# Causal attention with its scores made twice: once for the row maximum, once keys by queries with the maximum as two extra rows

## The chip, the core and the metric

One core of one Trainium2 chip runs the whole program. The core has five engines with queues of their own: PE (matrix products), DVE (vector), ACT (scalar), POOL and SP (here only a queue that starts DMAs). The metric is device time in microseconds (us); the median of three runs of the kernel before is 2293.73 us (2292.71 to 2295.2).

## The reference, cut to what matters

```python
def xattn(q, latent_kv, Wq, Wkv_expand, Wout):      # b=8, sq=512, H=512, 16 heads of 32
    qp = q @ Wq.T
    k, v = jnp.split(latent_kv @ Wkv_expand.T, 2, axis=-1)
    ...
    scores = jnp.einsum('bhqd,bhkd->bhqk', qh, kh) / sqrt(32)
    scores = jnp.where(tril, scores, finfo.min)      # causal
    attn = jax.nn.softmax(scores, axis=-1)
    return merge_heads(attn @ vh) @ Wout.T
x = x + xattn(layernorm(x), ctx_512, ...)
x = x + ffn(layernorm(x), ...)    # router of 8 experts per output column, top two, then the experts
```

Because of the causal mask only the first 512 of the 1601 context tokens matter. All is float32.

## The kernel before

The program has two stages. Attention runs first over 8 batches and stores x1; the router and the experts then run over 32 blocks of 128 tokens. The change touches the attention alone.

**Tiling.** A batch b has four chunks c of four heads each (128 of the 512 features); chunk n = 4b + c. A chunk has eight units v: unit v treats query block i = v // 2 (128 queries, keys 0 to 128(i+1), so 128 to 512 columns) of head pair v % 2. Per chunk PE makes the queries (Q, 4 x 3 products of 512 columns, L423) and the keys (K, 3 products, L434) as a high and a low float32r part, which ACT and DVE split (L693, L951). SP stacks the parts by 12 DMAs (`stack`, L280) into `qk_st`, so that one product over 96 rows gives the score to near float32 accuracy.

**One unit.** PE makes the scores of two heads, queries on partitions, and adds the mask by a product of bf16 tiles (L526, L529); two pairs of PSUM banks take turns. DVE takes the negated row maxima (L1021). ACT makes the exponentials with that maximum as its bias and with a running sum, one instruction a head (L740). Two units later (LAG) PE turns the probabilities, 128 x 128 at a time (`turn_probs`, L475), and ACT and DVE copy one head each into `pT` (L708, L968). When all eight units of chunk n-1 are turned, at unit v = 2 of chunk n, PE multiplies by the values (`values_of`, L486): four column tiles of 32 side by side, float32 in both operands. The reciprocals of the sums are taken on 16 numbers a partition (L974), spread to 512 (L978), turned by PE (L451), copied by ACT (L760) and multiplied in by DVE (`scaled`, L987). POOL splits the result (L1367, L1369).

**Order.** Every engine's queue is written out by hand and is in order. `fillers` (L238) says which other PE work stands in which unit: K at v = 0, Q at v = 1, the turned reciprocals R at v = 2; values V (3 products each) in chunk 0 at v = 4 to 7, the output projection WO (12 products each) in chunk 1 at v = 4 to 7, the turned layer norm LNT in chunk 2 at v = 4 to 7. K and Q are those of chunk n+1. `over_batches` (L261) writes batch 0 and batch 7 out and runs batches 1 to 6 in a hardware loop, so the loop is turned five times.

## Time and profile before

| | |
|---|---|
| median of three runs | 2293.73 us |
| the profiled execution | 2295.15 us, span 2293.1 us |
| attention, to the last product with values | about 0 to 720 us |
| PE busy over the span | 2173.1 us (95%) |
| DVE, ACT, POOL busy | 69%, 49%, 31% |
| mean granted TensorE clock | 0.986 |

Times in the rows are from the start of the span. Busy time of PE counts the latency of each product, so neighbouring products overlap in it; the pace is read from start to start. An idle time in brackets names who ended it; "issue" is a wait for nothing that the profile shows. A clock of 1.00 is 2.4 GHz, the other level is 1.2 GHz.

### The profile page before, as it was taken

The numbers are of one execution on the slowest core, as the hardware profiler recorded it, in microseconds if no ns is written. First come the engines' busy times: TensorE is split into PE (matmuls) and PEld (weight loads), VectorE is DVE, ScalarE is ACT, GpSimd is POOL, SyncE is SP. The second block draws the span as 40 slices with busy tenths as digits, with TensorE's granted clock in tenths as the row PEclk, the third lists the DMA queues.
The fourth block names the chain that finished last, engine by engine and source line by source line (L and its number), as shares of the span: only waits on it lengthen the run. The fifth ranks groups of instructions, "written<-read, shape, count | busy, mean of one in ns | idle before, by whom it ended". The sixth has DMA issues, their size and how long they took to land.

```text
span 2293.1 us, 37558 instructions
## 1 busy us (share of the span) xinstructions
PE 2173.1 (95%) x11264; PEld 1685.4 (73%) x11264; DVE 1591.9 (69%) x2844; ACT 1123.6 (49%) x3059; POOL 710.0 (31%) x669
## 2 busy tenths in 40 slices
PE   5998898998998999999999999987999999999999
PEld 4676676776775777777777777766888888888887
DVE  4775666756767899999999999997633434333433
ACT  4766656657666577777777777783200000000000
POOL 1330321312302465666556665652200000000000
PEclk9999999999999999999999999998999999999999
DMA  5444444435436000000000000040000000000000
GB/s 147 118 109 119 116 99 106 123 91 124 97 100 218 19 10 9 9 14 9 9 11 12 9 9 14 9 151 11 26 21 27 18 27 18 27 18 27 18 27 19
DMA packets 64106, 123.08 MB, mean 54 GB/s; under 512 B 8553, under 2 KB 8577, under 8 KB 64033
## 3 DMA queue, kind: packets, MB, share of 16 engines
q1 hardware_dynamic: 64032, 122.28, 19.6%
q8 instruction: 24, 0.39, 0.1%
q14 instruction: 50, 0.40, 0.1%
HBM read 55.12 MB, written 16.78 MB: 31 GB/s over the span
## 4 chain that ended last, share of the span: by engine, by line
PE 53%; DVE 19%; issue 18%; ACT 7%; DVEq 1%; SPq 1%; DMA 1%; POOL 0%; ACTq 0%; POOLq 0%
PE pair L227 11%; PE pair L229 11%; PE pair L228 11%; DVE ps L1209 4%; PE ps L475 4%; PE ps L486 3%; DVE top_b L1121 3%; PE ps L227 3%; ACT probs L740 3%; PE ps L228 3%; PE ps L229 3%; PE pair L526 2%; DVE top_b L1139 2%; DVE top_a L1131 2%; DVE scrap L1217 1%
## 5 line engine op out<-in xcount | busy, mean ns | idle before, releaser
L227 PE MATMUL pair<-w_h,hT_h 128*128 128x512 f32 x2048 | 855.1, 418 | 4.4 <-issue 2.7
L229 PE MATMUL pair<-w_h,hT_l 128*128 128x512 f32 x2048 | 803.1, 392 | 0.0
L228 PE MATMUL pair<-w_l,hT_h 128*128 128x512 f32 x2048 | 798.1, 390 | 0.0
L1296 DVE SCALAR_TENSOR_TENSOR xb<-pair,c_now,xb 128x512 f32<-128x512 f32 x256 | 192.1, 751 | 398.5 <-PE pair L229 398.0
L229 PEld LDWEIGHTS pair<-w_h,hT_l 128*128 128x128 f32 x2048 | 385.1, 188 | 86.8
L228 PEld LDWEIGHTS pair<-w_l,hT_h 128*128 128x128 f32 x2048 | 386.2, 189 | 80.4
L227 PEld LDWEIGHTS pair<-w_h,hT_h 128*128 128x128 f32 x2048 | 388.3, 190 | 75.5 <-issue 5.1
L1438 POOL TENSOR_TENSOR logits<-logits,second 128x512 f32<-128x512 f32 x256 | 323.5, 1306 | 134.2 <-DVE second L1153 134.2
L783 ACT ACTIVATE hT_h<-ps 128x512 fp32r<-128x512 f32 x64 | 38.3, 599 | 664.7 <-PE ps L583 664.7
L1377 POOL TENSOR_TENSOR rstd<-moments,eps 128x1 f32<-128x1 f32 x96 | 77.2, 804 | 844.3 <-DVE moments L924 844.3
L740 ACT ACTIVATE probs<-pair,nmax 128x384 f32<-128x384 f32 (+3 forms) x512 | 272.8, 556 | 33.5 <-DVE nmax L1021 33.5
L1021 DVE TENSOR_REDUCE nmax<-pair 128x2 f32<-128x256 f32 (+3 forms) x256 | 210.0, 820 | 83.7 <-PE pair L529 82.8
L475 PE MATMUL ps<-ident,probs 128*128 128x128 f32 x1280 | 194.2, 282 | 31.3 <-ACT pT L708 28.9
L1367 POOL TENSOR_TENSOR oT_h<-o_sb,zero 128x512 fp32r<-128x512 f32 x32 | 33.3, 1039 | 531.6 <-DVE o_sb L987 310.3
L708 ACT ACTIVATE pT<-ps 128x128 f32<-128x128 f32 (+3 forms) x256 | 118.9, 464 | 147.2 <-PE ps L475 124.7
L968 DVE COPY pT<-ps 128x128 f32<-128x128 f32 (+3 forms) x256 | 124.2, 485 | 96.1 <-PE ps L475 96.1
L526 PE MATMUL pair<-qk_st 96*128 96x384 f32 (+3 forms) x512 | 163.1, 377 | 24.4 <-ACT probs L740 13.7
L475 PEld LDWEIGHTS ps<-ident,probs 128*128 128x128 f32 x1280 | 138.5, 143 | 47.9 <-issue 34.2
L846 ACT ACTIVATE logits<-pair 128x512 f32<-128x512 f32 x256 | 145.3, 583 | 29.2 <-PE pair L229 29.1
L1209 DVE SCALAR_TENSOR_TENSOR ps<-logits,ps 128x512 f32<-128x512 f32 x217 | 148.9, 686 | 3.7 <-POOL logits L1438 0.4
L1217 DVE SCALAR_TENSOR_TENSOR scrap<-ps,w 128x512 bf16<-128x512 f32 x217 | 145.0, 678 | 0.0
L803 ACT ACTIVATE over<-logits 128x512 f32<-128x512 f32 x224 | 133.1, 623 | 15.3 <-POOL logits L1438 15.2
(150 smaller groups left out, 3176.2 us busy)
## 6 DMA issues: line engine op xcount, KB each, us to landing
qk_st<-qk SPq DMA_DIRECT2D x384, 128.0 KB, 2.4
xb<-x SPq DMA_DIRECT2D x64, 256.0 KB, 2.7
xt<-in_x SPq DMA_DIRECT2D x8, 1024.0 KB, 7.8
xr<-in_x SPq DMA_DIRECT2D x8, 1024.0 KB, 5.4
x<-xr SPq DMA_DIRECT2D x8, 1024.0 KB, 4.3
w_raw<-in_routerT SPq DMA_DIRECT2D x8, 1024.0 KB, 11.8
w_raw<-in_expertT SPq DMA_DIRECT2D x8, 1024.0 KB, 5.8
out_dram<-xb SPq DMA_DIRECT2D x32, 256.0 KB, 2.0
```

The source lines that it names most:

```text
L227: pe.matmul(dst, lh, rh, start=start, stop=False)
L228: pe.matmul(dst, lh, rl, start=False, stop=False)
L229: return pe.matmul(dst, ll, rh, start=False, stop=stop)
L475: mm = pe.transpose(t_ps[j][:, kb * P:(kb + 1) * P], probs[:, k, j, kb * P:(kb + 1) * P], ident[:])
L526: pe.matmul(bank[:, 0:w], qk_st[c % 2][0:STACK, hh, 0, i * P:w], qk_st[c % 2][0:STACK, hh, 1, 0:w], start=True, stop=False)
L740: e = act.activation(probs[:, k, j, 0:w], s_ps[slot][:, j, 0:w], ACT.Exp, bias=nmax[:, k, j:j + 1], accum_out=sums[:, c % 2, i, hh:hh + 1])
L846: act.activation(logits[i][:, e, :], l_ps[e % 4], ACT.Copy).then_inc(s["lg_ok"], 1)
L1021: dve.tensor_reduce(nmax[:, k, :], s_ps[slot][:, :, 0:w], AX_X, ALU.max, negate=True)\
L1209: dve.scalar_tensor_tensor(taken[(e + 1) % slots], lg[:, e, :], 0.0, taken[e % slots], ALU.is_equal, ALU.add).then_inc(s["count"], 1)
L1217: dve.scalar_tensor_tensor(scrap[:, e % 2, :], taken[e % slots], 1.0, w2[:], ALU.min, ALU.mult, accum_out=c_taken[:, i, e - 1:e]).then_inc ...
L1296: dve.scalar_tensor_tensor(xb[i][:], l_ps[e % 4], c_now[i][:, e:e + 1], xb[i][:], ALU.mult, ALU.add).then_inc(s["acc"], 1)
L1438: pool.tensor_tensor(logits[i][:, e, :], logits[i][:, e, :], second[:], ALU.subtract)\
```

## The change

The order of the attention is written anew. In words:

- Scores are made in two passes. Pass one (`scores`, on PE) is as before, but into one pair of banks, with the mask as float32r tiles, largest query block first; DVE takes the maxima (`maxima`). It runs one chunk and two units ahead (LEAD). The next unit's scores wait until the maxima are taken.
- After the eight maxima PE turns the [128, 16] tile of maxima (`turn_maxima`). ACT and DVE split it into a high and a low part, and ACT starts two DMAs that put them as rows 96 and 97 into `qk_st` (`shift_rows`, `lo_shift`). The keys' side holds ones there.
- Pass two (`shifted_scores`) makes keys by queries over 98 rows, for key block kb = v // 2 and queries 128kb to 512. ACT takes one exponential over two heads straight into `pT`, with no sum and no bias (`exps`). POOL zeroes the future in the diagonal block (`hide_future`). Turning the probabilities and its copies go.
- The product with values comes in four pieces, one a key block (PV 0 to 2 at v = 4, 6, 7, PV 3 at v = 1 of the next chunk), and each piece has a second product with a tile of ones, [128, 32] for each head, which leaves the sums in the layout of the output (`d_ps`). DVE takes the reciprocal of that [128, 512] tile and multiplies (`reciprocals`, `scaled`).
- Q, K and their stack run three chunks ahead (AHEAD) into four `qk_st` tiles. Q stands at v = 0 to 3, K at v = 5; V at v = 0 to 3 and LNT at v = 4, 6, 7 of chunk 0; WO half a block a unit at v = 0 to 7 of chunk 1. POOL normalizes a batch earlier.
- The loop runs batches 1 to 5; 0, 6 and 7 are written out.

```diff
-LAG = 2
+LEAD = 2
+AHEAD = 3
 STACK = 3 * HD
+SHIFT_ROWS = 2
...
-        probs = att("probs", [P, 4, 2, S], F32)
+        qk_st = [att(f"qk_st{i}", [P, 2, HC, S], F32R) for i in range(KC)]
         pT_at = att.at
-        pT = att("pT", [P, HC, QB, S], F32)
+        pT = [att(f"pT{kb}", [P, HC, S - kb * P], F32) for kb in range(QB)]
-        r_sb = att("r_sb", [P, S], F32)
-        r_rep = att("r_rep", [P, QB, HC, HD], F32)
-        recip = att("recip", [P, QB, HC], F32)
-        sums = att("sums", [P, 2, QB, HC], F32)
-        nmax = att("nmax", [P, 4, 2], F32)
+        nmax = att("nmax", [P, 2, HC * QB], F32)
+        nm_h = att("nm_h", [P, P], F32R)
+        nm_l = att("nm_l", [P, P], F32R)
+        mask_raw = att("mask_raw", [P, P], F32)
+        ident_r = att("ident_r", [P, P], F32R)
+        mask_r = att("mask_r", [P, P], F32R)
+        ones = att("ones", [P, HD], F32)
...
-        s_ps = pairs
-        t_ps = ps[0:2]
+        s_ps = pairs[0]
+        e_ps = pairs[1]
+        r_ps = pairs[0][0:HC * QB, 0, S - P:S]
         j_ps = ps[2:4]
-        o_ps = j_ps[0]
+        o_ps = ps[0]
+        d_ps = ps[1]
...
+        def target(c, v):
+            k = v + LEAD
+            return 1 + k // UNITS, k % UNITS
+        def block_of(v):
+            return QB - 1 - v // 2
         def fillers(c, v, first, last):
             found = []
-            if v == 0 and not (last and c == KC - 1):
+            if v < KC and not (last and c > 0):
+                found.append(("Q", v))
+            if c == 0 and v < QB:
+                found.append(("V", v))
+            if v == 5 and not (last and c > 0):
                 found.append(("K", None))
-            if v == 1 and not (last and c == KC - 1):
-                found.append(("Q", None))
-            if v == 2 and not (first and c == 0):
+            if c == 1 and not first:
+                found.append(("WO", v))
+            return found
+        def openers(c, v, first, last):
+            found = []
+            if v == 1 and not (first and c == 0):
+                found.append(("PV", QB - 1))
+            if v == 6 and not (last and c == KC - 1):
                 found.append(("R", None))
-            if c == 0 and v >= 4:
-                found.append(("V", v - 4))
-            if c == 1 and v >= 4 and not first:
-                found.append(("WO", v - 4))
-            if c == 2 and v >= 4 and not last:
-                found.append(("LNT", v - 4))
+            if v in (4, 6, 7):
+                found.append(("PV", (4, 6, 7).index(v)))
+            if c == 0 and not last:
+                found += [("LNT", i) for i in {4: (0,), 6: (1,), 7: (2, 3)}.get(v, ())]
...
-            with eng.Fori(1, B - 1) as b:
-                body(b, False, False)
-            body(B - 1, False, True)
+            body(0, True, True, True)
+            with eng.Fori(1, B - 2) as b:
+                body(b, False, True, True)
+            body(B - 2, False, True, False)
+            body(B - 1, False, False, False)
...
+                    if more or c == 0:
+                        stack(n + AHEAD, (c + AHEAD) % KC, b * 16 if c == 3 and not first else 0)
...
-            def turn_probs(u, k, v):
-                pe.wait_ge(s["exps"], u + 1)
-                i = v // 2
...
+            def scores(n, c, v):
+                u = n * UNITS + v
+                i, pair = block_of(v), v % 2
+                w = (i + 1) * P
+                if v < 2:
+                    pe.wait_ge(s[f"stacked{pair}"], (n + 1) * (16 * STACK_DMAS))
+                if v == 0 and some(n):
+                    pe.wait_ge(s["nm_hi"], n)
+                    pe.wait_ge(s["nm_lo"], n)
+                if some(u):
+                    pe.wait_ge(s["negmax"], u)
                 for j in range(2):
+                    hh = 2 * pair + j
+                    pe.matmul(s_ps[:, j, 0:w], qk_st[c][0:STACK, 0, hh, i * P:w], qk_st[c][0:STACK, 1, hh, 0:w],
+                              start=True, stop=False)
+                    mm = pe.matmul(s_ps[:, j, i * P:w], ident_r[:], mask_r[:], start=False, stop=True)
+                mm.then_inc(s["scores"], 1)
+            def turn_maxima(n, c):
+                pe.wait_ge(s["negmax"], (n + 1) * UNITS)
+                pe.transpose(r_ps, nmax[:, c % 2, :], ident[:])\
+                    .then_inc(s["turned"], 1)
+            def shifted_scores(n, c, v):
+                u = n * UNITS + v
+                kb, pair = v // 2, v % 2
+                w = S - kb * P
+                if v == 0:
+                    pe.wait_ge(s["rows_in"], (n + 1) * (16 * SHIFT_ROWS))
+                if some(u):
+                    pe.wait_ge(s["exps"], u)
+                for j in range(2):
+                    hh = 2 * pair + j
+                    mm = pe.matmul(e_ps[:, j, 0:w], qk_st[c][0:STACK + SHIFT_ROWS, 1, hh, kb * P:(kb + 1) * P],
+                                   qk_st[c][0:STACK + SHIFT_ROWS, 0, hh, kb * P:S], start=True, stop=True)
+                mm.then_inc(s["shifted"], 1)
+            def values_of(n, c, b, kb):
+                pe.wait_ge(s["causal"], n * UNITS + 2 * kb + 2)
+                pe.wait_ge(s["v_ok"], b * QB + kb + 1)
+                if kb == 0:
+                    if some(n):
+                        pe.wait_ge(s["o_ok"], n)
+                for hh in range(HC):
+                    h = c * HC + hh
+                    pe.matmul(o_ps[hh * HD:(hh + 1) * HD, kb * P:S], v_sb[:, kb, h * HD:(h + 1) * HD],
+                              pT[kb][:, hh, :], start=(kb == 0), stop=(kb == QB - 1),
+                              tile_position=(0, hh * HD), skip_group_check=True)
+                for hh in range(HC):
+                    mm = pe.matmul(d_ps[hh * HD:(hh + 1) * HD, kb * P:S], ones[:], pT[kb][:, hh, :],
+                                   start=(kb == 0), stop=(kb == QB - 1), tile_position=(0, hh * HD),
...
+                        for task, k in openers(c, v, first, last):
+                            if task == "R":
+                                turn_maxima(n + 1, c + 1)
+                            elif task == "PV":
+                                if k == QB - 1:
+                                    values_of(n - 1, (c - 1) % KC, b if c else b - 1, k)
+                                else:
+                                    values_of(n, c, b, k)
+                            else:
+                                take(lnt_bank(k), "LNT", (b + 1) * QB + k)
+                                norm_turn((b + 1) * QB + k, k, lnt_bank(k))
+                        shifted_scores(n, c, v)
+                        g, vv = target(c, v)
+                        if more or c + g < KC:
+                            scores(n + g, (c + g) % KC, vv)
...
+            def shift_rows(n, c):
+                act.wait_ge(s["turned"], n + 1)
+                if some(n * (16 * SHIFT_ROWS)):
+                    act.wait_ge(s["rows_in"], n * (16 * SHIFT_ROWS))
+                rows = slice(0, HC * QB)
+                act.activation(nm_h[rows, :], r_ps, ACT.Copy).then_inc(s["nm_hi"], 1)
+                act.wait_ge(s["nm_hi"], n + 1)
+                act.wait_ge(s["nm_lo"], n + 1)
+                for k, part in enumerate((nm_h, nm_l)):
+                    row = slice(STACK + k, STACK + k + 1)
+                    act.dma_start(f32(qk_st[c][row, 0].rearrange("p h (i q) -> p (h i) q", q=P)), f32(part[rows, :])).then_inc(s["rows_in"], 16)
...
+                        act.wait_ge(s["shifted"], u + 1)
+                        if some(n):
+                            act.wait_ge(s["pv"], (n - 1) * QB + kb + 1)
+                        act.activation(pT[kb][:, pair:pair + 2, :], e_ps[:, :, 0:S - kb * P], ACT.Exp, bias=zero[:])\
+                            .then_inc(s["exps"], 1)
...
+            def maxima(n, c, v):
+                u = n * UNITS + v
+                i, pair = block_of(v), v % 2
+                dve.wait_ge(s["scores"], u + 1)
+                if v == 0 and some(n - 1):
+                    dve.wait_ge(s["turned"], n - 1)
+                at = 2 * pair * QB + i
+                dve.tensor_reduce(nmax[:, c % 2, at:at + QB + 1:QB], s_ps[:, :, 0:(i + 1) * P], AX_X, ALU.max, negate=True)\
+                    .then_inc(s["negmax"], 1)
+            def lo_shift(n):
+                dve.wait_ge(s["nm_hi"], n + 1)
+                if some(n * (16 * SHIFT_ROWS)):
+                    dve.wait_ge(s["rows_in"], n * (16 * SHIFT_ROWS))
+                rows = slice(0, HC * QB)
+                dve.tensor_tensor(nm_l[rows, :], r_ps, f32(nm_h[rows, :]), ALU.subtract).then_inc(s["nm_lo"], 1)
+            def reciprocals(n):
+                dve.wait_ge(s["pv"], (n + 1) * QB)
                 if some(n):
                     dve.wait_ge(s["o_lo"], n)
+                dve.reciprocal(o_sb[:], d_ps[:]).then_inc(s["recips"], 1)
+            def scaled(n):
+                dve.wait_ge(s["recips"], n + 1)
+                dve.tensor_tensor(o_sb[:], o_ps[:], o_sb[:], ALU.mult).then_inc(s["o_ok"], 1)
...
+                            reciprocals(n - 1)
+                        if v == 2 and not (first and c == 0):
                             scaled(n - 1)
+                        for task, a in fillers(c, v, first, last):
+                            if task == "Q" and a == KC - 1:
+                                lo_of(n + AHEAD, QL, "q", 1)
+                            elif task == "K":
+                                lo_of(n + AHEAD, KL, "k", 1)
+                            elif task == "WO" and a % 2 == 1:
+                                residual(b - 1, a // 2, 0)
+                        if c == 2 and v % 2 == 1 and further:
+                            block_statistics(b + 2, v // 2)
...
+            def hide_future(u, kb, v):
+                pool.wait_ge(s["exps"], u + 1)
+                pair = 2 * (v % 2)
+                diag = pT[kb][:, pair:pair + 2, 0:P]
+                pool.affine_select(out=diag, in_=diag, compare_op=ALU.is_ge, fill=0.0, base=0,
+                                   pattern=[[0, 2], [1, P]], channel_multiplier=-1).then_inc(s["causal"], 1)
...
+                    for v in range(UNITS):
+                        hide_future(n * UNITS + v, v // 2, v)
+                        if v == 0 and c == 1 and more:
+                            split_context(b + 1)
+                        if v == (7 if c == 1 else 2) and not (first and c == 0):
+                            split_outputs(n - 1, (c - 1) % KC, b if c else b - 1)
+                        if further and (c, v) in ((2, 3), (2, 5), (2, 7), (3, 1)):
+                            norm_turned(b + 2, ((2, 3), (2, 5), (2, 7), (3, 1)).index((c, v)))
```

## Rows read from the trace of the kernel before

**Rows 1.** Busy time by stretch: us and count per engine, granted clock, DMA share, GB/s
```profile
97.00:114.60 17.60, 16.32 (x127) 11.63 (x131) 12.26 (x21) 12.81 (x44) 2.31 (x2) 1.00 0.74 203
...
202.10:221.00 18.90, 18.50 (x139) 13.65 (x141) 12.36 (x21) 14.53 (x48) 2.33 (x2) 1.00 0.45 98
221.00:247.40 26.40, 26.33 (x175) 20.21 (x175) 18.03 (x37) 13.51 (x44) 5.81 (x8) 1.00 0.38 99
247.40:266.30 18.90, 18.12 (x143) 13.51 (x145) 14.63 (x25) 14.45 (x48) 12.23 (x15) 1.00 0.39 84
266.30:290.50 24.20, 19.21 (x128) 13.90 (x131) 12.25 (x21) 13.00 (x44) 2.31 (x2) 0.86 0.55 153
```

**Rows 2.** Timeline where the loop turns: start, us, instruction, idle before
```profile
371.88 0.60 ACT L708 ACTIVATE pT<-ps 128x512 f32<-128x512 f32 x1 [4.43 <-issue]
...
372.62 1.94 PE L475 MATMUL ps<-ident,probs 128*128 128x128 f32 x8 [4.34 <-ACT pT L708]
```

**Rows 3.** Timeline of PE, chunks 1 to 3 of batch 3
```profile
414.17 0.40 PE L526 MATMUL pair<-qk_st 96*128 96x512 f32 x1
...
414.84 0.83 PE L475 MATMUL ps<-ident,probs 128*128 128x128 f32 x6
...
418.28 0.22 PE L526 MATMUL pair<-qk_st 96*128 96x128 f32 x1
...
418.61 1.04 PE L475 MATMUL ps<-ident,probs 128*128 128x128 f32 x8
...
419.41 0.48 PE L227 MATMUL ps<-ctx_h,wkv_h 128*128 128x512 f32 x1
...
421.31 0.48 PE L227 MATMUL ps<-xnT_h,wq_h 128*128 128x512 f32 x1
...
424.16 0.28 PE L526 MATMUL pair<-qk_st 96*128 96x256 f32 x1
...
424.69 2.36 PE L486 MATMUL ps<-pT,v_sb 128*32 128x512 f32 x32
...
426.98 0.44 PE L475 MATMUL ps<-ident,probs 128*128 128x128 f32 x2
```

**Rows 4.** Timeline: scores of 512 columns start on PE, their maxima on DVE
```profile
450.98 0.49 PE L526 MATMUL pair<-qk_st 96*128 96x512 f32 x1 [0.50 <-ACT probs L740]
...
451.94 1.23 DVE L1021 TENSOR_REDUCE nmax<-pair 128x2 f32<-128x1024 f32 x1 [0.67 <-PE pair L529]
```

**Rows 5.** Groups by form, 279 to 545 us: count | busy us, mean ns | idle before
```profile
L1021 DVE TENSOR_REDUCE nmax<-pair 128x2 f32<-128x1024 f32 x24 | 29.3, 1221 | 10.4 <-PE pair L529 10.4
L1021 DVE TENSOR_REDUCE nmax<-pair 128x2 f32<-128x256 f32 x24 | 10.1, 421 | 4.8 <-PE pair L529 4.6
...
L740 ACT ACTIVATION_READ_ACCUMULATOR probs<-pair,nmax 128x1 f32 x192 | 44.9, 234 | 0.0
L708 ACT ACTIVATE pT<-ps 128x512 f32<-128x512 f32 x24 | 15.8, 659 | 17.9 <-issue 13.0 <-PE ps L475 4.5
L708 ACT ACTIVATE pT<-ps 128x128 f32<-128x128 f32 x24 | 6.9, 285 | 29.0 <-PE ps L475 29.0
```

**Rows 6.** Groups by form of DVE, whole span: the reciprocal and two other small operations
```profile
L1254 DVE COPY c_pad<-c_hi 128x8 f32<-128x8 f32 x64 | 7.9, 169 | 0.0
L974 DVE RECIPROCAL recip<-sums 128x16 f32<-128x16 f32 x32 | 7.8, 243 | 0.0
L1173 DVE TENSOR_SCALAR c_taken<-th_sum 128x1 f32<-128x1 f32 x32 | 4.7, 146 | 0.0
```

**Rows 7.** Timeline of POOL at the start: a masked selection of 128 elements a partition
```profile
1.64 0.29 POOL L1346 TENSOR_SCALAR_AFFINE_SELECT ident<-ident 128x128 f32<-128x128 f32 x1 [0.25 <-POOL zero L1343]
```

**Rows 8.** Timeline of SP's queue: the twelve DMAs of one stack
```profile
444.74 7.78 SPq L295 DMA_DIRECT2D qk_st<-qk  x12
```

**Rows 9.** Timeline at the start: the second pair of heads is stacked
```profile
36.01 0.48 PE L526 MATMUL pair<-qk_st 96*128 96x128 f32 x1 [1.46 <-DMA qk_st<-qk]
```

**Rows 10.** Timeline of DVE behind the last product with values
```profile
720.38 0.69 DVE L987 TENSOR_TENSOR o_sb<-ps,r_sb 128x512 f32<-128x512 f32 x1 [4.78 <-PE ps L486]
```

445 lines of the change are left out of this document (187 added, 258 removed).

## The prediction

> **What bounds the kernel now.** I read the stretches first. Without a turn of the loop a batch takes 18.9 us (chunk 0), 26.4 (chunk 1), 18.9 (chunk 2) and 17.6 (chunk 3), 81.8 us in all, and PE is busy for nearly all of it [rows 1]. Only the attention, up to 720 us, changes; its span must give or take the whole difference. Where the loop turns, a chunk takes 24.2 us instead of 17.6, at a mean clock of 0.86: ACT sits 4.43 us on "issue", PE 4.34 us behind it [rows 2], and the rest is the half clock. That is 6.6 us a turn, five turns.
>
> Then the paces of PE, from start to start [rows 3]. A unit's two scores with their masks cost 0.67 us at 512 columns and 0.33 at 128 (I take 0.56 and 0.52 between); a turned 128 x 128 block 0.10 (eight in 0.80); Q 2.85 and K a quarter of it, 0.70 (three products); one V 0.70; the product with values of a chunk 2.29 us for 1280 columns of four heads, or 1.8 ns a column. A plain chunk (number 3) has Q, K, scores (4.2), 40 turned blocks (4.0), values and reciprocals (0.4): 14.4 us of work in 17.6. The other 3.2 us are hand-overs between PE, DVE and ACT.
>
> **PE's work, part by part, a chunk.** Gone: 40 turned probabilities 4.0 and four turned reciprocals 0.4. New: the second pass, 16 products without masks, 2 x (0.47 + 0.36 + 0.26 + 0.22) = 2.6 (128 columns is held by the weight load, so not a quarter of 512); the product with ones, another 2.3; cutting both into four pieces, about 0.3; float32r masks 0.2; the turned maxima 0.1. So -4.4 + 5.5: work goes up by 1.1 us, to 15.5. V, WO and LNT stay (2.8, 11.2 and about 2 us in their chunks).
>
> **ACT** loses 16 reads of the accumulator, its copies of pT and one copy a chunk, and gains one copy of 128 and two DMA starts; a DMA start on SP costs 7.78 / 12 = 0.65 us [rows 8], so I take 1.3. Its eight exponentials over both heads are taken like the copies without accumulator (0.285 at 128, 0.659 at 512, so 1.16 at 1024) [rows 5]. It ends well under PE. **POOL** gains eight selections of 256 elements; 0.29 us for 128 [rows 7] makes about 0.43 each, and the first pair has more than 8 us before its PV. SP's stack is the same 7.8 us; three chunks ahead it has room, and the row DMAs (starts by 2.3 us after the turned maxima, landing 2 to 2.5 later) end just inside the wait named next. Cover gone, each 1 us later costs 1 us a chunk.
>
> **What ends last: two chains.** PE's next scores now wait for the maxima before. For 512 columns, scores start, 0.96 us later DVE starts, and takes 1.23 [rows 4]: 2.2 us from one start to the next. At 384, 256 and 128 columns I get 1.8, 1.5 and 1.05 from the forms 1221 and 421 ns [rows 5]. For the exponentials the same sum gives 1.9, 1.55, 1.2 and 0.9. I walk one plain chunk with these floors (time 0: PE starts the last 512-column scores, v = 7). v=0: second pass at 0.67, scores at 2.2 (1.06 us lost), Q to 3.46. v=1: PV 3 to 4.03, scores 4.5, Q to 5.76. v=2: scores 6.3, Q to 7.5. v=3: scores 7.9, Q to 9.1. v=4: PV 0 (1.85) to 10.96, scores 11.2. v=5: scores 12.4, K to 13.55. v=6: maxima turned, PV 1 (1.4) to 15.1, scores 15.3. v=7: PV 2 (1.0) to 16.97, scores 17.5 by the floor. So 17.5 us, of which 2 are floors: what the turned probabilities cost in hand-overs comes back in another form.
>
> **The new reciprocal.** DVE's queue at v=1 is: maxima, reciprocal of [128, 512], (residual, statistics), then the maxima of v=2, on which PE's scores of v=3 wait. Before, 16 elements take 243 ns, one element in another operation 146 and a copy of eight 169 [rows 6]. If the surplus grows with the elements, (243 - 146) / 16 = 6.1 ns each, 512 take 3.3 us. If it is a fixed surplus, 512 take about 0.75, like a copy. Those are the two ends. I take 3.3: the row is nearest in kind, and a copy of 16 at about 1 ns an element leaves 70 ns to explain. The Trainium skill ("VectorE: DVE Perf Modes", Walkthrough: the 8-slice pipeline in each mode) says the reciprocal iterates a divide with a repeat count of 8; that speaks for the slow end, and its consequence is a rival below.
>
> With 3.3 us: maxima of v=1 end at 6.3, the reciprocal at 9.6, the maxima of v=2 at 10.3, so scores of v=3 start at 10.35 instead of 7.9: 2.5 us a plain chunk, 20.0 us. Chunk 2 adds a statistic (0.8) in the same place: 21.1. In chunk 0, V fills half of the gap; with V and LNT it is 23.0. In chunk 1 WO fills it but for the residual behind the reciprocal: 27.8. A batch: 23.0 + 27.8 + 21.1 + 20.0 = 91.9, against 81.8.
>
> **The sum, for the profiled execution.** Six batches x 10.1 = +60.6. Batch 0: its chunk 4 begins at about 108 before (its values start at 114.6, two units later [rows 1]). After, the eight units of maxima run alone before anything else: second pair of heads stacked at 36.0 [rows 9], maxima to 46.4, then rows, Q and K at half clock in part, first second pass at 54; plus 21 + 20.0 + 20.8 + 20.0 gives 136: +28. Batch 7 has no Q and K in three chunks and no maxima in the last: 76 against 84: -8. Tail: a reciprocal in the open against the half-clock product that ends at 720.4 [rows 10]: +1. One turn of the loop less: -6.6. Together +75: 2295 + 75 = 2370 us; profiled execution and median differ by 1.4 us, so I say **2368 us**.
>
> **The rivals.**
> 1. The reciprocal is as fast as a copy (0.75 us). Then chunks take 21.7, 26.3, 18.5 and 17.5 = 84.0, six times +2.2, batch 0 +20, batch 7 -13, tail -1, turn -6.6: +12, **2306 us**, with 2285 to 2325 about it. The base ALU rate in every other row speaks for it, the 70 ns against it.
> 2. Faster than before: the floors overlap more than I walked, with a fast reciprocal. The mechanism is PE's queue filling the gap behind each maximum; it decides once the reciprocal is under 0.9 us (then v=3 never waits) and the 512-column hand-over is nearer 1.1 than 2.2 us. Then PE's work alone counts: 4 x 15.5 + 2.8 + 11.2 + 2 = 78.0 a batch, six times -3.8, batch 0 +15, batch 7 -15, turn -6.6: **2264 us**. For it: chunk 1 takes 26.4 for 25.6 us of work [rows 1]. Against it: one pair of banks instead of two.
> 3. The divide passes each element eight times through DVE. One pass costs (1221 - 421) / 768 = 1.04 ns an element [rows 5], so 512 elements take 8 x 512 x 1.04 = 4.3 us; every chunk but the fully filled ones loses 1 us more, some 28 us in all: **2396 us**. Against it: 16 elements would take 133 ns and leave 110 ns fixed, less than the 146 of any row [rows 6]. By the figures of the Trainium skill ("Trainium Kernel Development and Optimization", NeuronCore Architecture: VectorE at 0.96 GHz) and the repeat count above, an estimate is 4.27 us; the row agrees in direction only.
> 4. Waits make PE fall to the half clock in each chunk, as behind the loop's turn, or the row DMAs land late: 1 to 3 us a chunk, **2430 us**. The chunks here with up to 3.2 us of scattered waits stay at 1.00 [rows 1].
>
> **How the numbers follow.** Forecast 0.56 (2335 to 2385), rival 1 0.18, rival 2 0.13, rival 3 0.08, rival 4 0.05. From 2285 to 2415 leaves out rival 2 and most of rival 4, under 0.2. A measurement tells about 0.2% (4.6 us) from no change: faster takes rival 2 and 0.05 of rival 1 (0.18), same 0.06 of rival 1 with a little beside it (0.07), slower the rest (0.75). That the change does not do what it says is no rival of weight: the order is written out.
>
> **What the profile after would show.** The reciprocal's row near 3300 ns (forecast), 750 (rivals 1, 2) or 4300 (rival 3). PE idle of about 2.5 us once a plain chunk before the scores of v=3, ended by DVE's maxima; idle of about 1 us before the 384-column scores. Stretches of 23, 28, 21 and 20 us; no rows for turned probabilities; second-pass groups summing to 2.6 us a chunk by pace; first second-pass product near 54 us; four loop turns of some 6 us. The router and expert stretches unchanged. The prediction is wrong if the reciprocal is short, if PE's idle ends on POOL (selections) or on a DMA (rows), or if the floors are not met because DVE starts sooner behind short products.

## The result and the profile after

The changed kernel takes 2433.66 us (median of 4 runs, 2430.13 to 2438.0) beside 2294.42 us for the kernel before on the same chip: a ratio of 1.0609, 95% interval 1.059 to 1.0627. It is slower by 139 us. I had said 2368, range 2285 to 2415: the direction is right, the place of the loss only in part, and the size is far too small. All executions were in the fast state but one of e13's four (3577.6 us at a clock of 0.557), without which e13's median is 2388.8 us instead of 2389.1.

The page of the changed kernel: span, busy time per engine, the chain that ended last, and two groups whose columns are count, busy, mean and idle before.

```profile
span 2428.4 us, 35549 instructions
...
PE 2242.1 (92%) x11360; PEld 1673.3 (69%) x11424; DVE 1579.8 (65%) x2588; ACT 959.6 (40%) x2035; POOL 819.6 (34%) x930
...
PE 54%; DVE 24%; issue 16%; ACT 4%; DMA 1%; DVEq 1%; ACTq 1%; POOL 1%; SPq 0%; POOLq 0%
...
L799 ACT ACTIVATE pT<-pair,zero 128x1024 f32<-128x1024 f32 (+3 forms) x256 | 203.1, 794 | 366.5 <-PE pair L515 324.8
...
L1476 POOL TENSOR_SCALAR_AFFINE_SELECT pT<-pT 128x256 f32<-128x256 f32 x256 | 104.0, 407 | 459.3 <-ACT pT L799 459.3
```

ACT and POOL are far from full and come out as costed (a selection 407 ns, where I had 430). DVE stands on the path instead. A group of DVE by form shows how, over the whole span:

```profile
L1030 DVE RECIPROCAL o_sb<-ps 128x512 f32<-128x512 f32 x32 | 107.2, 3348 | 16.5 <-PE ps L532 16.5
```

and two of PE by form:

```profile
L528 PE MATMUL ps<-pT,v_sb 128*32 128x512 f32 x256 | 44.1, 769 | 0.0
...
L492 PE MATMUL pair<-qk_st 96*128 96x256 f32 x128 | 38.8, 353 | 44.1 <-DVE nmax L1013 44.1
```

The reciprocal takes 3348 ns. The scores of 256 columns, which stand behind it (v=3), account for 44 us of PE idle time, all of it released by DVE's maxima. And the other row of PE is what I had not priced: a product with values of 512 columns, in the piece that comes after that wait, takes 769 ns in the mean, where e1 below, without the wait, has 633.

To see where 135.3 us of span come from, I cut the runs at the instruction in which DVE scales the output of a chunk (L987 before, L1035 after; 32 in each). This table is worked out from their start times; columns e1, e11, e12 and e13 are experiments below.

| stretch, us | before | after | e1 | e11 | e12 | e13 |
|---|---|---|---|---|---|---|
| start to chunk 0's | 63.5 | 101.5 | 98.7 | 93.6 | 96.0 | 65.3 |
| chunks 1 to 3 | 55.4 | 73.3 | 59.4 | 62.8 | 54.6 | 61.9 |
| six batches | 524.7 | 601.0 | 540.3 | 553.3 | 521.1 | 594.4 |
| last batch | 76.8 | 81.4 | 76.9 | 81.3 | 77.1 | 87.4 |
| the rest | 1572.7 | 1571.2 | 1572.5 | 1571.3 | 1572.5 | 1572.5 |
| span | 2293.1 | 2428.4 | 2347.8 | 2362.2 | 2321.2 | 2381.5 |

So: start +38.0, next three chunks +17.9, six batches +76.2, last batch +4.6, router and experts -1.5.

One batch of the changed kernel by chunks 0 to 3, each cut at that instruction, which runs at v=2 of the next chunk, so the windows lie that much late (us and count of PE, PEld, DVE, ACT, POOL, then the granted clock). It takes 101.3 us where the stretches of before give 81.8 [rows 1], without the loop's turn.

```profile
275.01:301.32 26.31, 22.55 (x159) 15.35 (x160) 14.87 (x20) 9.78 (x16) 7.82 (x12) 1.00 0.40 101
301.32:329.05 27.73, 25.03 (x166) 17.25 (x164) 14.70 (x20) 8.71 (x12) 5.52 (x10) 0.98 0.37 95
329.05:353.38 24.33, 20.23 (x128) 11.67 (x128) 14.27 (x24) 7.69 (x11) 16.59 (x26) 0.88 0.31 65
353.38:376.30 22.92, 21.01 (x137) 13.10 (x137) 11.87 (x14) 8.84 (x14) 5.52 (x10) 0.93 0.51 126
```

Chunks 2 and 3, which have the least work to fill waits with, are at a clock of 0.88 and 0.93.

**Where a chunk 2 stands still, in the timelines** (start, us, instruction, idle before it). First DVE:

```profile
426.26 0.96 DVE L1013 TENSOR_REDUCE nmax<-pair 128x2 f32<-128x768 f32 x1 [1.55 <-PE pair L494]
427.14 3.35 DVE L1030 RECIPROCAL o_sb<-ps 128x512 f32<-128x512 f32 x1
430.40 0.64 DVE L956 BATCH_NORM_STATS2 stats<-xt 128x6 f32<-128x512 f32 x1
...
431.30 0.69 DVE L1013 TENSOR_REDUCE nmax<-pair 128x2 f32<-128x512 f32 x1
```

Then PE in the same stretch:

```profile
432.05 0.39 PE L492 MATMUL pair<-qk_st 96*128 96x256 f32 x1 [2.85 <-DVE nmax L1013]
...
433.40 1.59 PE L528 MATMUL ps<-pT,v_sb 128*32 128x512 f32 x8
434.75 1.95 PE L532 MATMUL ps<-pT,ones 128*32 128x512 f32 x8
436.63 0.76 PE L515 MATMUL pair<-qk_st 98*128 98x256 f32 x2
...
440.01 0.85 PE L528 MATMUL ps<-pT,v_sb 128*32 128x384 f32 x8
440.68 0.83 PE L532 MATMUL ps<-pT,ones 128*32 128x384 f32 x8
```

The maxima that PE waits for start 0.81 us after the reciprocal's end, behind a statistic; PE stands for 2.85 us. Soon behind the wait the products run at the half clock: the first piece with values and its piece with ones take from 433.40 to 436.63, 3.23 us. The same pair at full clock takes 1.85 us (e5, below). By 440 the 384-column pieces have their full pace again: 0.67 us from start to start, about three quarters of the 512-column piece's 0.85 in e5. In chunk 3, which has no statistic, the wait is 1.89 us long (before 353.51, in the batch of the four rows above), and there too the half clock follows.

But it does not follow every such wait. In batch 1 the same place goes on at full clock:

```profile
230.61 0.39 PE L492 MATMUL pair<-qk_st 96*128 96x256 f32 x1 [2.84 <-DVE nmax L1013]
...
231.97 1.07 PE L528 MATMUL ps<-pT,v_sb 128*32 128x512 f32 x8
232.85 1.04 PE L532 MATMUL ps<-pT,ones 128*32 128x512 f32 x8
```

In the loop's batches 1 to 5 the half clock follows four of the five waits of chunk 2 (2.84 to 2.85 us) and three of the five of chunk 3 (1.87 to 1.89 us).

**The start** (PE's timeline):

```profile
33.00 0.47 PE L492 MATMUL pair<-qk_st 96*128 96x512 f32 x1 [2.94 <-DMA qk_st<-qk]
...
40.03 0.76 PE L492 MATMUL pair<-qk_st 96*128 96x512 f32 x1 [6.14 <-DVE nmax L1013]
...
65.23 1.17 PE L515 MATMUL pair<-qk_st 98*128 98x512 f32 x2
```

The first product of the second pass starts at 65.2 us; I had 54. The scores of chunk 0 run alone, one pair of banks, a DVE maximum between any two, and from the second unit to the turned maxima at half clock (a 512-column product 0.76 us long against the 0.40 of [rows 3]). The second unit itself starts late, at 40.03, because the first unit's maxima stand in DVE's order behind the splits of chunk 1's keys and queries, and these behind ACT:

```profile
37.46 0.69 DVE L1002 TENSOR_TENSOR qk<-ps,qk 128x512 fp32r<-128x512 f32 x1 [7.13 <-ACT qk L752]
...
38.66 1.22 DVE L1013 TENSOR_REDUCE nmax<-pair 128x2 f32<-128x1024 f32 x1
```

The scores for these maxima were made by 34 us.

### The profile page after: what moved, and what is told of

The parts are those of the page before. It is cut to its first block, busy times and chain, and to the rows that moved or that the text cites. A ratio compares the mean times of both kernels' runs of the same rounds, so it can differ in the third digit from the quotient of the medians.

```text
span 2428.4 us, 35549 instructions
## 1 busy us (share of the span) xinstructions
PE 2242.1 (92%) x11360; PEld 1673.3 (69%) x11424; DVE 1579.8 (65%) x2588; ACT 959.6 (40%) x2035; POOL 819.6 (34%) x930
## 4 chain that ended last, share of the span: by engine, by line
PE 54%; DVE 24%; issue 16%; ACT 4%; DMA 1%; DVEq 1%; ACTq 1%; POOL 1%; SPq 0%; POOLq 0%
PE pair L229 10%; PE pair L231 10%; PE pair L230 10%; DVE ps L1258 4%; PE pair L492 4%; DVE o_sb L1030 4%; PE ps L528 3%; PE pair L515 3%; DVE top_b L1170 3%; PE ps L532 3%; PE ps L229 3%; PE ps L231 2%; PE ps L230 2%; DVE nmax L1013 2%; DVE top_b L1188 1%
## 5 line engine op out<-in xcount | busy, mean ns | idle before, releaser
L1013 DVE TENSOR_REDUCE nmax<-pair 128x2 f32<-128x1024 f32 (+3 forms) x256 | 210.1, 821 | 267.6 <-PE pair L494 267.2
L799 ACT ACTIVATE pT<-pair,zero 128x1024 f32<-128x1024 f32 (+3 forms) x256 | 203.1, 794 | 366.5 <-PE pair L515 324.8
L1476 POOL TENSOR_SCALAR_AFFINE_SELECT pT<-pT 128x256 f32<-128x256 f32 x256 | 104.0, 407 | 459.3 <-ACT pT L799 459.3
L492 PE MATMUL pair<-qk_st 96*128 96x256 f32 (+3 forms) x512 | 167.5, 371 | 78.9 <-DVE nmax L1013 70.6
L492 PEld LDWEIGHTS pair<-qk_st 96*128 96x128 f32 x512 | 101.6, 199 | 107.9 <-DVE nmax L1013 82.1
L515 PE MATMUL pair<-qk_st 98*128 98x256 f32 (+3 forms) x512 | 145.3, 366 | 24.7 <-ACT pT L799 20.4
L515 PEld LDWEIGHTS pair<-qk_st 98*128 98x128 f32 x512 | 82.8, 195 | 109.1 <-issue 63.2
L852 ACT ACTIVATE over<-over 128x512 f32<-128x512 f32 x224 | 138.8, 623 | 1.0
```

The lines of the kernel that those rows point to most:

```text
L492: pe.matmul(s_ps[:, j, 0:w], qk_st[c][0:STACK, 0, hh, i * P:w], qk_st[c][0:STACK, 1, hh, 0:w], start=True, stop=False)
L515: mm = pe.matmul(e_ps[:, j, 0:w], qk_st[c][0:STACK + SHIFT_ROWS, 1, hh, kb * P:(kb + 1) * P], qk_st[c][0:STACK + SHIFT_ROWS, 0, hh, kb * P ...
L799: act.activation(pT[kb][:, pair:pair + 2, :], e_ps[:, :, 0:S - kb * P], ACT.Exp, bias=zero[:])\
L1013: dve.tensor_reduce(nmax[:, c % 2, at:at + QB + 1:QB], s_ps[:, :, 0:(i + 1) * P], AX_X, ALU.max, negate=True)\
```

## The experiments

My theory after the result was: the reciprocal's 3.35 us in DVE's order between two maxima costs the time, first as PE idle time, then a second time as a stretch at half clock. The rivals: the products with ones and the second pass are simply more work for PE; the row DMAs land late; the start costs most of it. In each, "before" is what was measured on the same chip beside it: 2295.88 us for e1 to e4, 2296.07 for e5 to e9, 2294.64 for e11 to e14. The differences to the changed kernel's 2433.66 are across chips, whose kernels before lie within 1.7 us of each other. Where I part a stretch into clock and idle, the change in PE's busy time at an equal number of products stands for the clock, and the rest is idle time.

**e1: a copy in the reciprocal's place** (the output is then multiplied by the sum instead of divided).

```diff
-dve.reciprocal(o_sb[:], d_ps[:])
+dve.tensor_copy(o_sb[:], d_ps[:])
```

> The changed kernel with the reciprocal of [128, 512] replaced by a copy (0.68 us on DVE instead of 3.35); so the output is divided by nothing, scaled by the sum instead. Theory A (the reciprocal holds up the maxima of v=2, PE idles 2.5 to 3.4 us, its clock falls and PV 0 runs at half clock for 1.4 us more): a batch falls from 100.7 to about 86 us, the whole by 32 x 3.7 = 110 to 130 us, to about 2310 us; the 512-column products with values back to some 600 ns. Theory B (the added products with ones and the second pass fill PE, the reciprocal only uses DVE's spare time): under 40 us less, above 2390 us.

Measured: 2349.41 us, ratio 1.0237 (1.022 to 1.0254). 84 us of the 139 go with one instruction a chunk. A batch of e1:

```profile
247.65:272.95 25.30, 22.89 (x164) 15.96 (x163) 12.49 (x20) 10.82 (x18) 7.84 (x13) 1.00 0.48 131
272.95:298.35 25.40, 25.27 (x167) 17.47 (x165) 12.07 (x21) 7.91 (x12) 5.91 (x11) 1.00 0.40 104
298.35:317.65 19.30, 16.99 (x127) 10.50 (x127) 11.74 (x24) 7.59 (x11) 14.52 (x24) 1.00 0.39 82
317.65:337.25 19.60, 18.55 (x136) 12.24 (x136) 9.33 (x15) 8.69 (x13) 7.06 (x12) 1.00 0.48 118
```

The clock is back at 1.00 in every chunk of this batch (three of the six batches show 0.98), and the batch is 11.7 us shorter than after's 101.3. These rows also part the two costs. PE does the same number of products within a few, so what its busy time shrank by is clock, and what is left is idle time: in chunk 2, 20.23 against 16.99 busy, that is 3.2 us of the 5.0 gained; in chunk 3, 21.01 against 18.55, 2.5 of 3.3. In chunks 0 and 1 busy time does not shrink, and the 1.0 and 2.3 us are idle time. Over the batch 5.1 us are clock and 6.6 are idle. Over all six batches PE's busy time goes from 528.1 to 506.3 us and its idle time from 72.8 to 34.0: of the 60.7 us gained there, 22 are clock and 39 idle. The gain is less than I expected, though: 54 us over the kernel before remain, so something else costs as well.

**e2: half of it.** 256 columns by reciprocal, 256 by copy (half of the output is not divided).

```diff
-dve.reciprocal(o_sb[:], d_ps[:]).then_inc(s["recips"], 1)
+dve.reciprocal(o_sb[:, 0:256], d_ps[:, 0:256]).then_inc(s["recips"], 1)
+dve.tensor_copy(o_sb[:, 256:512], d_ps[:, 256:512]).then_inc(s["recips"], 1)
```

> The changed kernel with the reciprocal taken of 256 columns and a copy of the other 256 (1.74 + 0.35 = 2.1 us on DVE instead of 3.35; half the output is scaled wrongly). Theory A with the clock as its second part: the idle before the scores of v=3 falls from 2.85 to about 1.3 us, short enough to keep the clock, so more than half of the gain of the full copy: 65 to 85 us less, 2350 to 2370 us. Theory A without the clock (plain waiting): in proportion, (3.35 - 2.1) x 24 chunks = 30 to 40 us less, about 2400 us. Theory B: under 15 us less.

Measured: 2371.81 us, 1.0332 (1.0315 to 1.0349): -62 us for half the dose, against -84 for all of it. Of the cost, the first 256 columns bring 22 us and the next 256 bring 62. PE's timeline in a chunk 2 of e2:

```profile
403.38 0.39 PE L492 MATMUL pair<-qk_st 96*128 96x256 f32 x1 [1.56 <-DVE nmax L1013]
404.74 1.70 PE L528 MATMUL ps<-pT,v_sb 128*32 128x512 f32 x8
406.19 1.95 PE L532 MATMUL ps<-pT,ones 128*32 128x512 f32 x8
```

Here 1.56 us of idle time are still followed by products at half clock, where I expected such a wait to keep the clock, and the gain stays short of the 65 to 85 us that went with that. Over the whole run such a product takes 684 ns in the mean (769 in after, 633 in e1), so fewer chunks have it. The bend in the dose is not the clock's. Over the six batches the first 256 columns (e1 to e2) add 11.3 us to PE's busy time and 10.9 to its idle time, the next 256 (e2 to after) add 10.6 and 27.9: only the idle time bends, as it would if a short delay is covered by other products.

**e5: the order of PE's work alone.** Nothing is taken away. At units 0 and 3 the fill work (Q, V, WO) goes ahead of the scores, so that PE has products to do while DVE is at the reciprocal.

```diff
-if more or c + g < KC:
+if v not in (0, 3) and (more or c + g < KC):
     scores(n + g, (c + g) % KC, vv)
 for task, k in fillers(c, v, first, last):
     ...
+if v in (0, 3) and (more or c + g < KC):
+    scores(n + g, (c + g) % KC, vv)
```

> The changed kernel with PE's other work of v=0 and v=3 (Q, V, WO) placed before that unit's scores instead of behind them; nothing is added or removed. In v=3 that puts 0.7 us or more into the idle behind the reciprocal, in v=0 into the 1 us behind the last maxima. If the idle is only a wait: 0.7 + 0.7 us in the plain chunks, less in chunks 0 and 1 where part is filled, 25 to 45 us less, 2390 to 2410 us, with the 512-column products with values still at half clock in 16 to 24 chunks. If the clock is the second part of the loss and an idle of 2.1 us keeps it: 1.4 us a chunk more, 50 to 80 us less, about 2365 us.

Measured: 2372.18 us, 1.0335 (1.0319 to 1.0351): -61.5 us with the same instructions. PE's timeline of a chunk 2, the same place as in after's timeline above:

```profile
401.00 0.39 PE L492 MATMUL pair<-qk_st 96*128 96x256 f32 x1 [2.22 <-DVE nmax L1015]
...
401.69 1.07 PE L528 MATMUL ps<-pT,v_sb 128*32 128x512 f32 x8
402.54 1.07 PE L532 MATMUL ps<-pT,ones 128*32 128x512 f32 x8
403.54 0.50 PE L515 MATMUL pair<-qk_st 98*128 98x256 f32 x2
```

then of the chunk 3 behind it, and the stretch around that:

```profile
421.32 0.39 PE L492 MATMUL pair<-qk_st 96*128 96x256 f32 x1 [1.26 <-DVE nmax L1015]
...
422.00 1.06 PE L528 MATMUL ps<-pT,v_sb 128*32 128x512 f32 x8
```

```profile
419.00:444.50 25.50, 23.71 (x171) 15.67 (x171) 15.93 (x18) 11.09 (x17) 9.99 (x16) 1.00 0.44 114
```

In chunk 2 the wait has shrunk from 2.85 to 2.22 us and in chunk 3 from 1.89 to 1.26, by 0.63 each, and the clock stays at 1.00: values and ones take 1.85 us in chunk 2 instead of 3.23, that is 1.4 less. Over a whole chunk 2 (by the same cuts) it is 20.3 us instead of 24.3. In batches 2 to 5 none of these waits is followed by the half clock; in batch 1 the 2.22 us of chunk 2 are. Over the six batches PE's busy time falls by 24 us and its idle time by 23, so a pure reordering brings back all of the clock that e1 brings back and part of the idle time. Whether the clock holds because the waits are shorter or because of the products now in front of them, no run here parts: after's chunk 3 lost it behind 1.87 to 1.89 us, e5's chunk 2 kept it behind 2.22. The wait that is left is the largest remaining one: the group of 256-column scores still has 28.2 us of idle time before it (44.1 in after).

**e13: the reciprocal alone, put into the kernel before.** The opposite test: the old kernel with one reciprocal of 128 x 512 more per chunk, at the place of its small one, in place on r_rep, which the next instruction overwrites.

```diff
 dve.reciprocal(recip[:], sums[:, c % 2]).then_inc(s["recips"], 1)
+dve.reciprocal(r_rep[:], r_rep[:]).then_inc(s["extra"], 1)
 dve.tensor_copy(r_rep[:], recip[:].unsqueeze(3).broadcast_to(...))
```

> The kernel before with one reciprocal of 128 x 512 more in each chunk, at the place between two maxima where it does its small one (in place on a buffer that is then overwritten, so the result is the reference's). If 3.35 us in DVE's order between two maxima is a cost of its own, whatever the rest of the chunk does, this loses 50 to 110 us (31 chunks by 1.6 to 3.5 us, idle and half clock together): 2345 to 2405, with a PE idle time of 2 to 3 us on the release of a maximum in each plain chunk. If only the changed kernel's schedule is that tight, under 20 us: below 2316.

Measured: 2389.09 us, 1.0414 (1.0395 to 1.0433): +94 us on the kernel before, without a second pass or a product with ones. DVE and then PE in a plain chunk:

```profile
391.56 3.29 DVE L978 RECIPROCAL r_rep<-r_rep 128x512 f32<-128x512 f32 x1
...
395.30 0.68 DVE L960 TENSOR_TENSOR qk<-ps,qk 128x512 fp32r<-128x512 f32 x1
...
396.49 0.68 DVE L1025 TENSOR_REDUCE nmax<-pair 128x2 f32<-128x512 f32 x1
```

```profile
396.08 2.36 PE L486 MATMUL ps<-pT,v_sb 128*32 128x512 f32 x32 [2.13 <-issue]
```

I had expected this wait at a maximum. The profile names no releaser; PE goes on 0.10 us after the end of DVE's first split behind the reciprocal (395.98) and before the maximum starts, so it is the split that it seems to wait for. All such waits before the products with values sum to 55.9 us (0.5 before). Its stretches by chunks, each from one chunk's scaled output to the next, the second with a turn of the loop and the fourth with WO in it:

```profile
379.46:400.53 21.07, 18.20 (x140) 13.70 (x139) 17.64 (x27) 14.47 (x48) 4.73 (x5) 1.00 0.28 59
400.53:427.19 26.66, 19.78 (x124) 13.92 (x123) 15.28 (x24) 12.96 (x45) 2.30 (x2) 0.81 0.49 137
427.19:448.35 21.16, 18.56 (x136) 13.66 (x135) 15.47 (x24) 14.49 (x49) 2.32 (x2) 1.00 0.41 92
448.35:478.62 30.27, 28.07 (x172) 21.06 (x171) 20.95 (x40) 13.50 (x45) 13.36 (x18) 0.94 0.38 98
```

The chunks of 18.9 us [rows 1] now take 21.1 and 21.2, by a wait of 2.1 to 2.2 us; the clock holds there. The chunk with WO goes from 26.4 [rows 1] to 30.3, with a clock of 0.94: there the products with values behind the same 2.13 us (at 472.54) take 3.9 us instead of 2.36. Over the six batches, 19 of the 69.7 us lost are PE's busy time, that is clock, and 51 idle time. So the price is not a property of the changed kernel's tight schedule, as a rival had it: 3.3 us more in DVE's in-order queue cost it in either kernel. Only one place in the old kernel was tried. That it costs the old kernel 94 and the new one 84 is no difference to build on, as the two wait in different places.

**e8: the reciprocal moved.** ACT copies the sums and the product with values out of PSUM, and DVE takes the reciprocal from the copy behind unit 3's maxima and fill work.

```diff
-if v == 1 and not (first and c == 0):
-    reciprocals(n - 1)
+if v == 3 and not (first and c == 0):    # behind maxima, fill work, statistics
+    reciprocals(n - 1)                    # reads d_sb, which ACT copied at v == 1
```

(The scaling moves from v=2 to v=4 and POOL's split behind it.)

> The changed kernel with the same reciprocal, 3.35 us, but of a copy in SBUF: ACT copies the sums and the product with values out at v=1 and v=2 (0.6 us each), PV 0 waits for these copies, and DVE takes the reciprocal behind the maxima of v=3, where PE has Q and PV 0 before it needs the next maxima, and multiplies at v=4. If place in DVE's queue is what costs, and not the 3.35 us themselves: as good as the copy instead of the reciprocal or better, 2335 to 2360 us, the output divided as in the changed kernel. If the length costs wherever it stands (DVE or its port to PSUM as a bound): 2400 us or more.

Measured: 2413.6 us, 1.0506 (1.049 to 1.0522): -20 us where I expected -75 to -100 if the place were what costs. It is the other case, 2400 us or more, in which the length costs at the new place too. PE's timeline in a chunk 3:

```profile
440.65 1.06 PE L530 MATMUL ps<-pT,v_sb 128*32 128x512 f32 x8
...
443.86 0.51 PE L517 MATMUL pair<-qk_st 98*128 98x256 f32 x2 [0.46 <-ACT pT L808]
445.81 0.33 PE L494 MATMUL pair<-qk_st 96*128 96x128 f32 x1 [1.44 <-DVE nmax L1026]
...
448.26 1.42 PE L530 MATMUL ps<-pT,v_sb 128*32 128x384 f32 x8
```

The gap at v=3 is gone and its pieces run at full clock. But the maxima of v=4 are now behind the reciprocal; PE waits before the 128-column scores of v=5 instead, where the units are shortest, and it is now the 384-column piece that runs at half clock. The idle time before the 128-column scores sums to 34.4 us (1.3 in after), that before the 256-column scores to 1.8 (44.1 in after). The stall moved with the instruction.

**e14: moved, with fill work before it** (e8, with the fill work of units 0 and 5 ahead of their scores, and e9's start).

> The reciprocal moved behind unit 3's maxima (with its sums and products copied out of PSUM by ACT), the fill work of units 0 and 5 ahead of their scores, and the reordered prologue. If the moved reciprocal lost only because the stall went to unit 5, where no work stood between, this gains 45 to 75 on the 2413.6 of the moved reciprocal alone: 2340 to 2370. If the small units after it cannot hide it whatever the order, 2390 to 2405.

Measured: 2383.14 us, 1.0398 (1.038 to 1.0416). That is 30 us better than e8 and between the two expectations. At v=5 only one projection is there to fill with, and 17.5 us of idle time before the 128-column scores remain, with 598 ns a 384-column product against 518 in e12. The fair neighbour is e11 below, measured on the same chip with the same start: 2366.5 us. So the reciprocal's old place with fill work before the scores is the better one, by 17 us.

**e3: no product with ones** (the reciprocal is then taken of the product with values; the output is not the reference's).

```diff
-for hh in range(HC):
-    mm = pe.matmul(d_ps[...], ones[:], pT[kb][:, hh, :], ...)
```

> The changed kernel without the products with ones; the reciprocal, as long as before, is taken of the product with values instead, so the sums are left out. Theory A: the removed PE work (2.4 us a chunk, 1.4 of it in the pieces v=4 and v=6 that wait for nothing) gives 1.5 to 2.6 us a chunk, 50 to 85 us, about 2350 to 2385 us; the reciprocal's idle stays at 2.85 us. Theory B: the full work and the hand-overs behind it, 85 us or more, under 2350 us.

Measured: 2407.21 us, 1.0488 (1.0471 to 1.0506): -26 us, less than either theory had, though 41.9 us of PE's busy time went away with the 512-column pieces alone. The group of 512-column scores says where the rest went:

```profile
L492 PE MATMUL pair<-qk_st 96*128 96x512 f32 x128 | 57.5, 499 | 26.3 <-DVE nm_l L1018 13.8 <-DVE nmax L1009 8.1 <-DMA qk_st<-qk 3.0
```

The idle time before them is 26.3 us; in after it is 16.3. The product takes 499 ns in the mean (460 in after), and the run's clock is 0.953 instead of 0.972. At v=3 the idle time falls only from 44.1 to 37.6 us. With less to do, PE waits longer for DVE elsewhere and gets a lower clock. PE's work alone is not what bounds the chunk.

**e4: rows of -30 in place of the maxima's rows**, written once by POOL; no row DMAs (the shift is then a constant instead of the row's maximum).

```diff
-for k, part in enumerate((nm_h, nm_l)):
-    act.dma_start(f32(qk_st[c][row, 0]...), f32(part[rows, :])).then_inc(s["rows_in"], 16)
```

> The changed kernel without the 64 row DMAs: both extra rows of the queries hold a constant written once, so the exponentials are shifted by a constant instead of the row maximum; the maxima, their turn and their split are still made. Theory A: only batch 0 shows waits for these DMAs (3.7 to 4.2 us at three places, against a floor that would hold most of it), and ACT loses 1.1 us of DMA starts a chunk that lie beside PV 1: 5 to 20 us less, 2415 to 2430 us. Theory C (the rows land late in most chunks): 1.5 to 3 us a chunk, 50 to 95 us less.

Measured: 2417.48 us, 1.053 (1.0512 to 1.0547): -16 us. The amount is theory A's, the place is not. The chain that ended last in after has three of these DMAs, all in batch 0, of 3.7 to 4.2 us each. But cut as in the table, e4's batch 0 is only 2.5 us shorter (100.3 and 72.0 us); the six batches are 9.1 us shorter, 6.3 of them in PE's busy time (a clock of 0.97 against 0.96). PE's own idle time on these DMAs is 3.9 us in all of after. What the six batches gain from, ACT's DMA starts or something else, no run here shows.

**e9: the start reordered.** The queries of chunk 2 go between the scores of units 3 to 6 of the first chunk.

```diff
 for v in range(UNITS):
     scores(0, 0, v)
+    if v == 3:
+        freed("Q", 1)
+    if 3 <= v < 3 + KC:
+        queries(2, 2, v - 3)
 turn_maxima(0, 0)
-freed("Q", 1)
-for k in range(KC):
-    queries(2, 2, k)
```

> The changed kernel with Q of chunk 2 moved from behind the eight first units of scores into the gaps of units 3 to 6; nothing added or removed. The first second-pass product starts at 65.2 us, 11 us later than I had summed. If the gaps and the half clock (Q of chunk 2 takes 4.5 us there) make the prologue long: it starts 5 to 7 us earlier, and the whole is 5 to 7 us shorter, 2427 us. If batch 0 is bound later by the stacks or the rows anyway: no change within 2 us.

Measured: 2422.96 us, 1.0558 (1.0542 to 1.0574): -10.7 us. The first product of the second pass starts at 61.45 instead of 65.23, so 3.8 us come from there, less than the 5 to 7 I expected, and the rest later.

**e11: both reorderings** (e5 and e9).

> The changed kernel with both reorderings: the fill work of units 0 and 3 ahead of their scores, and the queries of chunk 2 between the prologue's scores. If the two gains (61.5 and 10.7 us) lie in different stretches they add: 2355 to 2366. If the prologue's gain was clock that the loop now gives back anyway, 2368 to 2375. In neither case does it come below the kernel before (2296).

Measured: 2366.5 us, 1.0317 (1.0303 to 1.0331). It gains 5.7 us on e5 (about 4 if each is taken against its own chip's kernel before), about half of e9's 10.7, half a microsecond outside the range for gains that add. It is the fastest form of the changed kernel that computes the reference, and 72 us behind the kernel before.

**e12: a copy for the reciprocal, and e5's order** (output not divided). What is left of the loss without either part?

> Copy in place of the reciprocal, and the fill work ahead of the scores at units 0 and 3 (the output is then not divided by the right sum). If the copy alone has already taken away every gap that drops the clock in a plain chunk, the order is worth nothing more: 2343 to 2352. If gaps remain at the other units, 2320 to 2340. Only a value under 2300 would say that the second pass itself costs nothing.

Measured: 2321.37 us, 1.0114 (1.0099 to 1.013), 28 us under e1: so gaps did remain at other units. Its batch, with e11's beside it:

```profile
237.07:323.51 86.44, 82.78 (x590) 56.87 (x589) 45.24 (x74) 34.58 (x53) 35.31 (x58) 1.00 0.46 113
```

```profile
248.48:340.69 92.21, 83.80 (x589) 56.80 (x589) 55.29 (x73) 34.59 (x53) 35.31 (x58) 1.00 0.43 106
```

Both at clock 1.00. In the table, e12's six batches take 521.1 us against 524.7 before, its last batch and the rest are equal within 0.3; its only loss is the start, +32.5. That the six batches come out level is not because the second pass costs nothing, and by my own sign (under 2300) it does cost. The kernel before pays five turns of the loop in its 524.7. Without a turn its batch is 81.8 us [rows 1]; e12's is 86.4 and no longer where the loop turns (86.3 to 86.5 in batches 1 to 5). So the second pass with its extra rows and the product with ones cost about 4.6 us a batch more than what they replace, at full clock and without the reciprocal, and the turns that this kernel does not pay for give it back. Between e12 and e11, whose batches differ by 5.8 us at the same clock, stands the reciprocal as a plain delay.

**e7: the kernel before with one turn of the loop less** (the loop over batches 1 to 5, batch 6 written out).

```diff
-with eng.Fori(1, B - 1) as b:
+with eng.Fori(1, B - 2) as b:
     body(b, False, False)
+body(B - 2, False, False)
```

> The kernel before, with batch 6 written out and the loop over batches 1 to 5: one turn of the loop less, nothing else. If a turn costs the 6.6 us read from its stretch: 6.6 us less, ratio 0.9971. If the cost moves to the end of the loop or the instructions of the added batch are fetched late: no change, 0.999 to 1.001.

Measured: 2285.28 us, 0.9952 (0.9938 to 0.9965). One turn is worth 10.8 us (8 to 14 by the interval; 7.8 between the two profiled executions) where I had read 6.6, and this version beats both kernels: 0.5%, clear of the noise but small.

## Why the prediction was wrong, point by point

**The miss of 66 us in two parts.** Forecast and rival 1 differ by the reciprocal alone, 2368 against 2306: I had it at 62 us, and e1 measures 84. The other 43 us are there without it: e1 takes 2349 where rival 1 had 2306. So the larger part of the miss is not the reciprocal's. By the table, e1 against rival 1's terms is 19 us over in batch 0, 9 in the six batches and 13 in the last batch.

**The reciprocal's length: right.** 3.3 us expected, 3348 ns measured; 107.2 us in 32. One row of 16 elements beside two of its size was enough, and neither a fixed surplus (0.75, rival 1) nor eight passes (4.3, rival 3) came. The Trainium skill ("VectorE: DVE Perf Modes", Walkthrough: the 8-slice pipeline in each mode) gives the divide a repeat count of 8: right in direction; the measured slope, (3348 - 243) / 496 = 6.26 ns an element, is six times the 1.04 of one pass and not eight.

**The stall that follows: right in place, a little large.** I had 2.5 us in a plain chunk and 3.3 with the statistic of chunk 2; 1.89 and 2.85 came, released by DVE's maxima as expected.

**The clock behind the stall: the step that failed in the reciprocal's term.** I priced a stalled chunk at full clock and gave rival 4 a chance of 0.05, because a chunk of before with waits in it held 1.00 [rows 1]. Those waits are hand-overs, scattered over the chunk; here one wait takes the most of it. The products behind it ran at half clock and cost 3.2 us in chunk 2 and 2.5 in chunk 3 of the batch shown (e1's rows against after's), 22 us over the six batches. e5 shows that the instruction need not cost the clock: same instructions in another order, clock 1.00, -61.5 us. Rival 4 came nearest by its number, 2430, and that is luck: it was a round 1 to 3 us a chunk, the clock took less than 1 us a chunk over the six batches, and rival 4 had none of the 43 us above.

**The size of a batch: too small.** I walked 23.0, 27.8, 21.1 and 20.0; 26.3, 27.7, 24.3 and 22.9 came. In chunks 2 and 3 the misses of 3.2 and 2.9 us are about the clock's 3.2 and 2.5, but other errors cancel there: I had the waits 0.5 to 0.6 us too long, and e1 at full clock is still 0.8 and 2.1 us over my walk with a short reciprocal. In chunk 0 the 3.3 us are not: its clock is 1.00, and e1 misses my walk with a short reciprocal (21.7) by 3.6 there as well. For one part of that a row stands: the second pass costs by its starts in e5's batches about 0.57 us a unit at 512 columns, 0.35 to 0.46 at 384, 0.34 at 256 and 0.25 to 0.36 at 128 (from 403.54 on, for one, 0.34), some 3.2 us a chunk where I had 2.6. For another, order: e12 has chunk 0 at 24.4. The rest of chunk 0's miss I can't assign. Without the reciprocal my batch was 84.0; e1 takes 89.6 and e12 86.4.

**The loop's turn: wrong twice.** I subtracted one turn of 6.6 us and left four in the changed kernel. In the kernel before a turn is worth 10.8 (e7). In the changed kernel no chunk is longer for it: the chunks 3 between 252 and 776 us take 21.3 to 22.9 us with or without a turn behind them. For the six batches I had 54 us (six times 10.1, less 6.6); 76.2 came, 100.2 us a batch against 87.5 with the turns in. So two errors cancel: 100.2 against my 91.9 is 50 us too little over six batches, and the four turns of 6.6 that did not come hide 26 of it.

**Batch 0: +28 expected, +56 found** (38.0 and 17.9). This is the largest single term of the miss, and the second step that failed: I walked the start as if nothing else stood in DVE's order and at nearly full pace. The second pass starts 11 us late, 65.2 instead of 54. Of that, 4.0 us are the second unit's start (40.03 instead of 36.0, behind DVE's splits), 4.3 are the serial units from there to the turned maxima, 14.7 us instead of 10.4, at half clock, and the rest is the work behind them. The chunks after it have the stall and the clock (0.88 over the chunks 1 to 3, where e1 has 0.97). The row DMAs, which I thought of as rival 4's other half, are worth 2.5 us there (e4). That the start is a cost of its own, e12 shows: its span is 28.1 us over before's, with +32.5 in the start and -4.4 in the other stretches.

**The last batch: -8 expected, and +1 for the last reciprocal in the open; +4.6 found.** The last reciprocal does stand in the open, behind DVE's wait:

```profile
853.84 3.36 DVE L1030 RECIPROCAL o_sb<-ps 128x512 f32<-128x512 f32 x1 [11.37 <-PE ps L532]
```

In e1, without reciprocals, the same stretch is 76.9, as before: so they cost 4.5 us in this batch, and the 8 that I took away for the missing Q, K and maxima never came. With less work PE has a clock of 0.90 over this stretch, and 0.87 in e1, against 0.98 before, so the low clock is not the reciprocal's; that it eats the 8 us fits, but I made no run for it.

**Product with ones: its work right, its worth wrong.** 2.3 us a chunk of work is 74 us in 32 chunks; leaving it out gave 26 (e3). Adding up PE's work decides little where PE waits for another engine.

What stays open: some 2 us of chunk 0, the last batch's clock, what decides whether the half clock follows a wait, what e4 gains in the six batches, and why the changed kernel pays nothing for the loop's turn.
